# Spreading the experts' weights over partitions: one store and eight broadcast loads in place of zero-one products and copies

## The reference

```python
# attention: 16 heads of 8 features, scale 128 ** -0.5
q, k, v = split_heads(x @ Wq), split_heads(x @ Wk), split_heads(x @ Wv)
attn = softmax(q @ k.T * scale) + bias            # bias: from rel_table, added behind the softmax
out = layernorm(attn @ v, eps=1e-3) * gamma + beta
x = layernorm(x + out)
# feed-forward: 32 experts, each token takes its best 4
sim = (x @ hasher_w.T) @ keys.T                   # 32 similarities of each token
w = softmax(top_k(sim, 4))                        # 4 weights of each token
out = sum over its 4 experts of  w_n * (silu(x @ values_down[n]) @ values_up[n])   # 128 -> 32 -> 128
x = layernorm(x + x + scale * out ...)            # residual, then the last layernorm
```

## Time and profile before

| | |
|---|---|
| median of 3 runs | 302.82 us (298.81 to 302.82) |
| the profiled execution | 301.16 us; its span, first to last instruction, 299.1 us |
| busy share of the span | TensorE 93%, VectorE 79%, ScalarE 66%, GpSimd 44% |
| mean granted TensorE clock | 0.994 of full speed (2.4 GHz) |
| bytes moved by DMA | 17.27 MB, a mean of 58 GB/s |

### The profile page before, as it was taken

How to read it: one execution, slowest core, us unless ns; L and a number is a source line. 1 busy time by engine, 2 the same in 40 slices (tenths; PEclk the granted TensorE clock), 3 DMA queues, 4 the chain that set the end, 5 groups by cost and what they waited for, 6 DMA issues and landing times.

```text
span 299.1 us, 10998 instructions
## 1 busy us (share of the span) xinstructions
PE 278.4 (93%) x4660; PEld 146.7 (49%) x4661; DVE 235.5 (79%) x517; ACT 197.6 (66%) x390; POOL 130.9 (44%) x218
## 2 busy tenths in 40 slices
PE   4969999999999989999999999999999999889992
PEld 2644433444434344444557554445565645367482
DVE  4767899989989978987787799987977864148854
ACT  3652487867776668689864876889656689941620
POOL 8476133110115641137556312189365031885852
PEclk9997999999999999999999999999999999999999
DMA  5565095264051202000403030006100000010011
GB/s 158 154 179 150 9 182 118 40 178 118 2 136 31 79 4 83 4 2 25 139 6 81 4 83 5 1 3 177 24 4 2 6 3 3 2 37 2 2 37 35
DMA packets 18574, 17.27 MB, mean 58 GB/s; under 512 B 6830, under 2 KB 16222, under 8 KB 18526
## 3 DMA queue, kind: packets, MB, share of 16 engines
q1 hardware_dynamic: 17856, 16.39, 21.6%
q10 hardware_dynamic: 670, 0.19, 0.3%
HBM read 12.18 MB, written 4.23 MB: 55 GB/s over the span
## 4 chain that ended last, share of the span: by engine, by line
PE 68%; DVE 12%; DMA 6%; ACT 5%; POOL 4%; issue 3%; SPq 1%; POOLq 0%; DVEq 0%
PE sm_ps L1256 16%; PE st_ps L1256 14%; PE ov_ps L1311 14%; PE mi_ps L1256 6%; PE si_ps L1256 5%; DVE neg_max L947 5%; DMA k_stack<-parts_dram 3%; ACT probs L801 2%; DMA wq_sb<-L_attn_Wq 2%; ACT w_rows L703 1%; PE si_ps L1336 1%; PE mi_ps L1318 1%; PE st_ps L1568 1%; PE sm_ps L1336 1%; PE st_ps L1442 1%
## 5 line engine op out<-in xcount | busy, mean ns | idle before, releaser
L947 DVE TENSOR_REDUCE neg_max<-sm_ps 128x1 f32<-128x512 f32 x256 | 166.4, 685 | 29.2 <-PE sm_ps L1256 24.9
L801 ACT ACTIVATE probs<-st_ps 128x512 f32<-128x512 f32 x256 | 138.2, 610 | 34.0 <-PE st_ps L1256 34.0
L1256 PE MATMUL sm_ps<-k_stack,q_stack 96*32 96x512 bf16 x984 | 97.1, 383 | 3.0 <-DVE neg_max L947 2.1
L1256 PE MATMUL st_ps<-q_stack,k_stack 128*32 128x512 bf16 x1024 | 88.6, 380 | 0.2 <-ACT probs L801 0.2
L1311 PE MATMUL ov_ps<-probs,v_cur 128*32 128x256 f32 x1024 | 76.4, 378 | 0.0
L1256 PEld LDWEIGHTS sm_ps<-k_stack,q_stack 96*32 96x32 bf16 x984 | 26.3, 94 | 50.6 <-DVE neg_max L947 33.9
L533 POOL TENSOR_TENSOR hid<-hid,w_rows 128x512 f32<-128x512 f32 x27 | 34.1, 1278 | 30.7 <-ACT w_rows L703 30.7
L1311 PEld LDWEIGHTS ov_ps<-probs,v_cur 128*32 128x32 f32 x1024 | 31.6, 110 | 22.7 <-ACT probs L801 0.4
L1256 PEld LDWEIGHTS st_ps<-q_stack,k_stack 128*32 128x32 bf16 x1024 | 27.7, 96 | 28.3 <-ACT probs L801 9.1
L1010 DVE SCALAR_TENSOR_TENSOR hid<-tanh_sb,mi_ps 128x512 f32<-128x512 f32 x24 | 16.3, 681 | 15.0 <-ACT tanh_sb L838 15.0
L1256 PE MATMUL mi_ps<-x_t,down_sb 128*32 128x512 f32 x192 | 25.1, 592 | 0.0
(11 more groups left out here) (189 smaller groups left out, 301.2 us busy)
## 6 DMA issues: line engine op xcount, KB each, us to landing
q_stack<-parts_dram SPq DMA_DIRECT2D x16, 288.0 KB
k_stack<-parts_dram SPq DMA_DIRECT2D x48, 96.0 KB
parts_dram<-parts SPq DMA_DIRECT2D x24, 128.0 KB, 2.4
x_sb<-L_attn_x SPq DMA_DIRECT2D x4, 256.0 KB, 4.6
out<-y_out SPq DMA_DIRECT2D x3, 256.0 KB, 2.3
down_sb<-L_ffn_values_down SPq DMA_DIRECT2D x1, 512.0 KB, 5.7
up_sb<-L_ffn_values_up SPq DMA_DIRECT2D x1, 512.0 KB, 7.9
rel_win<-rel_dram SPq DMA_DIRECT2D x1, 256.0 KB, 2.7
```

The costliest lines, as they stand in the source:

```text
L801: nc.scalar.activation(probs[:, u % 2, j, :], st_ps[:, score_bank(u * J + j), :], ACT.Exp, scale=SCORE_SCALE).then_inc(probs_ready, 1)
L947: nc.vector.tensor_reduce(neg_max[:, g % 2, col:col + 1], sm_ps[:, c % 2, :], AX.X, ALU.max, negate=True).then_inc(max_ready, 1)
L1256: i = nc.tensor.matmul(dst[n * TILE:(n + 1) * TILE], weights[:, n * TILE:(n + 1) * TILE], moving, **flags)
```

## The change

In rounds 1 to 3, `wt` turns `w_tok` itself: four products with the identity, f32, into 128 partitions (chunk by expert) of `si_ps`; ScalarE copies these 128x128 values to `w_cols` and issues one store of 64 KB to `w_dram` in DRAM. The jobs `w0` to `w7` leave TensorE's stream. On ScalarE's queue they become eight loads of 256 KB, each with its own semaphore: the four rows of four experts, 2 KB each, every row to 32 partitions. The first of them waits for the store. They stand later in the job tables than the copies did. GpSimd's `split_weights` stays for the tail alone; all eight `weigh` now stand behind `split_shift(t+1, 0)` and the third fetch of values, and each waits for its load. `share` waits for the copy of the round before (long past).

```diff
+        w_dram = nc.dram_tensor("w_dram", [B - 1, NE, C, P], F32, kind="Internal").ap()
...
-                11: (["wt", "down4"], ["w1"]), 12: (["w0"], ["down5"]), 13: (["w2"], ["down6", "w3"]),
-                14: (["shift0", "w4"], ["down7", "w5"]), 15: (["w6"], ["w7"])}
+                11: (["wt", "down4"], []), 12: ([], ["down5", "w0"]), 13: (["w1"], ["down6", "w2"]),
+                14: (["shift0", "w3"], ["down7", "w4"]), 15: (["w5"], ["w6", "w7"])}
...
-                     11: ([], ["wt", "down4"]), 12: (["w0"], ["down5", "w1"]), 13: (["w2"], ["down6", "w3"]),
-                     14: (["w4"], ["w5"]), 15: (["shift0", "w6"], ["down7", "w7"])}
+                     11: ([], ["wt", "down4"]), 12: ([], ["down5"]), 13: (["w0"], ["down6", "w1"]),
+                     14: (["w2"], ["w3"]), 15: (["shift0", "w4"], ["down7", "w5", "w6", "w7"])}
...
-                    pool.wait_ge(side_done, job(t, f"w{j}", is_side))
+                    pool.wait_ge(w_loaded[j], 16 * t)
...
-                if experts:
-                    split_weights(f)
-                    for j in range(SHIFT_AFTER):
-                        weigh(f, t, j)
                 if attention:
                     if more:
                         split_shift(t + 1, 0)
                         fetch_values(t + 1, 2)
                     if experts:
-                        for j in range(SHIFT_AFTER, FJ):
+                        for j in range(FJ):
                             weigh(f, t, j)
...
+                    if f:
+                        act.wait_ge(w_stored, 16 * f)
+                    copy(w_cols[:], si_ps[:, 0:P]).then_inc(side_done, 1)
+                    act.wait_ge(side_done, job(t, name, is_side))
+                    nc.scalar.dma_start(w_dram[f].rearrange("e c q -> c e q"), w_cols[:]).then_inc(w_stored, 16)
+                elif name in LOADED:
                     j = int(name[1:])
-                    act.wait_ge(side_ready, job(t, name, is_side))
-                    if t > 1:
-                        act.wait_ge(weighed, hidden_count(f - 1, j))
-                    copy(w_rows[:, j], si_ps[:]).then_inc(side_done, 1)
+                    if j == 0:
+                        act.wait_ge(w_stored, 16 * t)
+                        if f:
+                            act.wait_ge(weighed, hidden_count(f - 1, FJ - 1))
+                    nc.scalar.dma_start(w_rows[:, j, :], bass.AP(w_dram.tensor, (f * NE + j * NJ) * S,
+                                                                 [[S, NJ], [0, PD], [1, S]])).then_inc(w_loaded[j], 16)
...
+                        if t < B:
+                            i = nc.tensor.matmul(si_ps[c * NE:(c + 1) * NE, 0:P], w_tok[:, c, :], ident[:],
+                                                 start=True, stop=True)
+                            continue
...
-                elif name in SPREAD:
-                    pe.wait_ge(side_done, job(t, "wt", is_side))
-                    i = spread_weights(bank[:, :], int(name[1:]))
```

More of the change, by code:

```diff
@@ L103, in bass_postln_attention_product_key_ffn @@
         spread = sb("spread", [PARTS * NE, FJ, NJ, PD], BF16)
-        w_rows = sb("w_rows", [P, FJ, S])
+        w_rows, w_cols = sb("w_rows", [P, FJ, S]), sb("w_cols", [C * NE, P])
         tanh_sb = sb("tanh_sb", [P, 3, S])
@@ L146, in bass_postln_attention_product_key_ffn @@
         spread_made, w_split, w_chain = sem("spread_made"), sem("w_split"), sem("w_chain")
+        w_stored, w_loaded = sem("w_stored"), [sem(f"w_loaded{j}") for j in range(FJ)]
         tail_spread, tail_copied = sem("tail_spread"), sem("tail_copied")
@@ L176, in bass_postln_attention_product_key_ffn @@
                      8: ([], ["down1"]), 9: (["shift3", "o0"], ["down2"]), 10: ([], ["down3"]),
[2 rows of a table removed]
[2 rows of a table added]
         TAIL_JOBS = {0: (["o1"], [f"up{j}" for j in range(FJ)]), 5: ([], ["x1t"]), 6: (["sim"], []), 11: ([], ["wt"])}
         OWN = ("shift0", "shift1", "shift2", "shift3", "o0")
-        SPREAD = tuple(f"w{j}" for j in range(FJ))
-        SIDE = ("o0", "wt", f"up{FJ - 1}") + SPREAD
-        SHIFT_AFTER, NORM_AFTER = 2, 3
+        LOADED = tuple(f"w{j}" for j in range(FJ))
+        SIDE = ("o0", "wt", f"up{FJ - 1}")
+        NORM_AFTER = 3
         PLACES = dict(attend=(0, 3), stats_a=(1, 3), stats_b=(4, 0), top=(7, 3), late_y=(8, 3), weights=(9, 1),
@@ L196, in is_misc @@
         def is_misc(n):
-            return n[:2] != "up" and n not in SIDE
+            return n[:2] != "up" and n not in SIDE + LOADED
         def is_kept(n):
@@ L213, in here @@
         def here(n, attention, experts, more, late):
-            if n in SPREAD and not attention:
+            if n in LOADED and not attention:
                 return False
@@ L537, in split_weights @@
                 pool.wait_ge(dve_step, dve_at(f, "w"))
-                if f:
-                    pool.wait_ge(side_ready, job(f, "wt", is_side))
-                    apart(pool)
                 nc.gpsimd.tensor_copy(w_parts[:, :, 0, :], w_tok[:]).then_inc(w_chain, 1)
-                pool.wait_ge(w_chain, f * 3 + 1)
+                pool.wait_ge(w_chain, 1)
                 nc.gpsimd.tensor_sub(w_res[:], w_tok[:], w_parts[:, :, 0, :]).then_inc(w_chain, 1)
-                pool.wait_ge(w_chain, f * 3 + 2)
+                pool.wait_ge(w_chain, 2)
                 nc.gpsimd.tensor_copy(w_parts[:, :, 1, :], w_res[:]).then_inc(w_chain, 1)
-                pool.wait_ge(w_chain, f * 3 + 3)
+                pool.wait_ge(w_chain, 3)
                 nc.gpsimd.tensor_sub(w_parts[:, :, 2, :], w_res[:], w_parts[:, :, 1, :]).then_inc(w_split, 1)
@@ L827, in expert_copy @@
                     act.wait_ge(side_ready, job(t, name, is_side))
[L828 to L834 removed]
+                    if t == B:
+                        copy(w_t[:], si_bf[0:PARTS * NE, 0:S]).then_inc(side_done, 1)
+                        return
+                    if f:
[4 more added lines that the diff above has]
+                elif name in LOADED:
+                    j = int(name[1:])
+                    if j == 0:
[4 more added lines that the diff above has]
+                                                                 [[S, NJ], [0, PD], [1, S]])).then_inc(w_loaded[j], 16)
                 else:
@@ L1040, in share @@
                 after(f, "wsum")
+                if f:
+                    dve.wait_ge(side_done, job(f, "wt", is_side))
                 step(nc.vector.reciprocal(winv[:], wsum[:]))
@@ L1515, in jobs @@
                     for name in half:
-                        if here(name, *kind):
+                        if here(name, *kind) and name not in LOADED:
                             misc(t, name, kind)
```

11 lines of the change are left out of this document (6 added, 5 removed), and 4 rows, old and new, of the table SECOND_JOBS.

## The result

The changed kernel takes 344.01 us (median of 4 runs, 343.55 to 344.69); the kernel before took 301.9 us beside it (298.81 to 302.82). The ratio is 1.1417, with a 95% interval of 1.1327 to 1.1508: slower by 14%. The profiled execution of after took 344.09 us with a span of 342.2, that of before 301.16 with 299.1, so the spans account for the difference: 43.1 us.

What follows compares the result with a forecast made beforehand. TensorE and ScalarE were taken as fullest, but GpSimd's multiplies, waiting for four-engine loads, decide: 301.2 + 37.4 of stalls - 2 gain + 3 lower clock = 339 us, own range 322 to 362 (wider range 306 to 368).

Steps and rivals of the forecast that it cites:

- Engines per load: Loads on ScalarE's queue: source's outermost dimension 4 decides, so four DMA engines a load, 132 packets.
- Rate: Loads in rounds 1 to 3: 23.1 GB/s an engine, 2.84 us a load (2.57 to 3.62), eight 22.7 us.
- Stalls: Ends of rounds 1 to 3: statistics or tail wait for late loads, 12.7, 12.4 and 12.3 us, sum 37.4.
- the term of the two slices: Rounds 1 and 2: SyncE's two slices on the same engines add 4.3 us to the loads, making 27.0.
- Lower clock and gain: TensorE's clock after three stalls costs 3 us; work saved before each round's first load gains 2 us.
- the row I went by (0.73): Before's profile: after 5 us with TensorE busy 2.96, granted clock 0.73 for 5 us, costing up to 1.35 us.
- The store's wait: Store in unit 11, about 5 us ahead of the first load: ScalarE's wait for it costs nothing.
- The exchange of transposes for f32 products: TensorE: twelve bf16 transposes a round become four f32 products; costed at nothing, at most 1.6 us in all.
- Loads in time: Rival, rounds 1 to 3: loads on 16 engines or within issue spacing land in time, faster or no change; 14%.
- my 291 to 307: Loads-in-time rival's times: 291 to 298 if half an issue overlaps the activation before it, 307 if none; rival 14%.
- A hot place in the measure of `gamma_sb`: Rival, loads' DRAM source: 8 KB served at 40 GB/s, 6.6 us a load, stalls about 42 us, 427 us; 6%.
- ScalarE held at the issue: Rival, `w5` to `w7`: full queue delays exponentials, 0 to 6 us on top, 339 to 345; within the forecast's 74%.

Runs made afterwards that it cites:

- sixteen engines: Changed kernel with each load bringing one expert of four groups, outermost dimension 32 instead of 4, same places and bytes: 329.82 us, ratio 1.0954.
- two engines: Changed kernel with each load cut into two of two experts, outermost source dimension 2, 16 issues a round: 410.27 us, ratio 1.3573.
- The four-engine kernel with earlier issues: Changed kernel with its own loads issued in units 12 and 13 (round 3: 12 to 14): 336.62 us, ratio 1.1169.
- Rows of their own: Kernel with outermost dimension 32, loads at the old places, each load reading 128 different rows of input x: 325.27 us, ratio 1.0769.
- the early sixteen-engine kernel: Changed kernel with outermost dimension 32 a load and issues in units 12 and 13 (round 3: 12 to 14): 306.33 us, ratio 1.0168.

## Why the prediction was right

**Engines per load.** Four, from the packets: 132 a load, 144 with 32 outermost, and the pace of the multiplies halved with 2. The Trainium skill, DMA: Bandwidth & Descriptors, "Why a DMA increments its semaphore by 16 and not by 1", lets both sides' slowest dimension decide. The source's 4 against the destination's 128 partitions was the case that no row of before had, and these counts agree.

**Rate.** 2.67 us a load (24.5 GB/s an engine), between the predicted 2.57 and 2.84.

**Stalls.** Predicted 12.7, 12.4 and 12.3, as delays of the statistics and the tail against each round's own first issue. Measured the same way: 14.5, 14.75 and 12.54. The statistics predicted at 164.2 were seen at 164.15, but by errors that cancel: the first load was issued at 131.08 and not at 133.0, and the way from the first issue to the last landing was 30.3 us, not 28.4. Its parts: the first load needed 5.14 us and not 4.24; seven more at 2.67 are 18.7, not 19.9; the two slices added 6.5 (4.28 and 2.21 in the two long gaps), not 4.3. Round 2 had 30.8 us. Round 3, without slices, was right. So **the term of the two slices was too small** by 2.2 to 2.8 us a round; the load's own term was a little too large.

**Lower clock and gain.** The forecast had a gain of 2 us, and the first issue stood 1.9 us early. That is luck: 1.2 us of it stood at round 1's bias addition, ahead of the change, and 0.6 come from an issue that ran beside the tanh of ScalarE and not behind it. In rounds 2 and 3 no gain shows: from the statistics to the next round's first issue, after took 0.9 us longer than before (208.38 - 164.15 against 194.9 - 151.54), then 1.2 (285.21 - 241.92 against 255.8 - 213.69), and 1.15 behind the tail's start. These 3.2 us answer to the 3 that were forecast for the clock. TensorE's clock after the three stalls (0.61, 0.57, 0.69) was lower than the row I went by (0.73). That row is no sure sign: in the execution of after TensorE was busy 3.29 us in the same 15 to 20, and the clock of 20 to 25 was 1.00. Shift writes landed late beside the loads, and TensorE's weight loads waited 4.1 and 3.8 us for two of them, but inside the stalls, ahead of the statistics. So they are no part of the 3.2; that all of it is the clock isn't shown.

**The sum.** 344.09 against 339; the prediction's own terms add up to 339.6. Stalls 41.8 in place of 37.4, an issue 1.9 us earlier in place of a gain of 2, 3.2 in place of 3. The clock and the earlier issue came out as forecast, the second by luck, so what is missing, some 4.4 us, lies in the stalls, and there in the slices.

**Costed at nothing.** The store's wait: in round 3 its bytes had moved 2.2 us after its issue, and the first load followed the store by 4.7, 5.0 and 3.9 us in the three rounds; it cost nothing. The exchange of transposes for f32 products: not measured alone; without the loads the kernel is 6 us faster in all, so it hides no large price.

**Rivals.** Loads in time: refuted by 132 packets, and with sixteen engines the loads at those places were still late, by the second limit, which neither that rival nor my 291 to 307 knew of. A hot place in the measure of `gamma_sb`: refuted by 2.67 us a load in place of 6.6, and a milder one by two engines (410) and sixteen (330). ScalarE held at the issue: it happened, at `w6` and `w7` (in round 3 from `w5` on):

```profile
140.82 8.86 ACTq L839 DMA_DIRECT2D w_rows<-w_dram  x2
```

8.86 us in round 1, 5.58 and 3.54 later. The chain of waits says what that cost, in order of time:

```profile
140.81 0.60 ACT probs L797
141.41 0.80 ACTq L839
142.21 0.03 issue
142.24 19.02 DMA w_rows<-w_dram
```

The chain leaves ScalarE's queue after 0.80 us and goes through the loads: in the shadow of the landings, as the rival's price of 0 to 6 said. The four-engine kernel with earlier issues shows it again.

## What to carry to other kernels

Before a spread by DMA takes the place of work on an engine, write down the outermost dimension of both sides, above all of the side that repeats. Here a source dimension of 4 or 2 gave as many engines, and 32 gave sixteen. Hold bytes / (engines x 24 GB/s) against the time until the first reader, and expect less of sixteen engines (14 to 15 GB/s each here); the idle share of DMA says nothing about it. Then look who stands behind the reader in a strict stream. More engines and an earlier start brought 38 of 43 us back, and 3 of the rest lay in an order that nobody would touch for the DMA's sake: a normalization that stood behind late data and could stand ahead of it. And before two traces are compared at a landmark, compare them at one ahead of the change.

## What the runs showed that I had not expected

- Sixteen engines spreading 2 KB rows take 119 to 128 ns a packet (14 to 15 GB/s each), four take 86 to 90. Rows of their own: 118 to 127. That limit is unexplained; whether it lies in the 32 partitions that a load writes is untested.
- Two slices beside four-engine loads cost these 6.5 to 7.1 us, though they bring only 2 x 49 KB to an engine (4.3 us at 23.1 GB/s).
- An issue of a four-engine load, whose sides differ in shape, cost 0.52 to 0.58 us on ScalarE's queue, not SyncE's 0.80, and one of a sixteen-engine load, whose sides agree, 0.31 to 0.35; which of the two differences counts isn't separated. It can run beside the activation ahead of it (issue at 131.08, tanh at 131.07).
- ScalarE's queue holds the issuing engine once some loads are outstanding: with four engines and early issues five went through and the sixth was held, each of them 33 packets an engine. Of the loads with 9 packets an engine, none was held as long: the longest issue in the early sixteen-engine kernel's three rounds took 1.2 us.
- Round 3's store of `y_out` landed after 6.2 us beside the loads; the median of this store was 2.3 before.
- The same start of the program ran at different clocks: in 20 to 25 us the granted clock was 0.66 to 0.76 in seven of the twelve traces and 1.00 in five, and round 1's bias addition came later with the lower clock, by 0.9 to 2.4 us between two traces.
